# Transposed copies of x and context in DRAM, and the keys contracted over rows of 512 weights

## The reference

```python
def reference(x, ctx_4096, g_xattn, g_ffn, ...):
    def _L0_xattn_ref(text, features, Wq_w, Wq_b, Wk_w, Wk_b, fn_w, qn_w, kn_w):
        features_n = rmsnorm(features, fn_w)
        Q = jnp.einsum('btd,fd->btf', text, Wq_w) + Wq_b
        K = jnp.einsum('bsd,fd->bsf', features_n, Wk_w) + Wk_b
        Q = rmsnorm(Q, qn_w)
        K = rmsnorm(K, kn_w)
        scores = jnp.einsum('btf,bsf->bts', Q, K) * scale
        attn = jax.nn.softmax(scores, axis=-1)
        return jnp.einsum('bts,bsf->btf', attn, features_n)
    def _L0_ffn_ref(x, ...):
        base = jnp.einsum('bsd,od->bso', x, W_base) + b_base
        ...
        return base + moe.reshape(base.shape)
    x = x + jnp.tanh(g_xattn[0]) * _L0_xattn_ref(_layernorm(x, axis=-1), ctx_4096, ...)
    x = x + jnp.tanh(g_ffn[0]) * _L0_ffn_ref(_layernorm(x, axis=-1), ...)
    return x
```

## Time and profile before

| | us |
|---|---|
| median of 3 runs | 528.93 |
| lowest and highest | 528.06, 531.78 |
| the profiled execution, its own time | 526.89 |
| its span, first to last instruction | 525.1 |

### The profile page before, as it was taken

How to read it: one execution, slowest core, us unless ns; L and a number is a source line. 1 busy time by engine, 2 the same in 40 slices (tenths; PEclk the granted TensorE clock), 3 DMA queues, 4 the chain that set the end, 5 groups by cost and what they waited for, 6 DMA issues and landing times.

```text
span 525.1 us, 7062 instructions
## 1 busy us (share of the span) xinstructions
PE 500.9 (95%) x2768; PEld 459.6 (88%) x2768; DVE 271.2 (52%) x584; ACT 153.0 (29%) x323; POOL 153.4 (29%) x123
## 2 busy tenths in 40 slices
PE   2589999999999999999988999999999999999997
PEld 2589888888888888888888999999999999999997
DVE  3887543525352532156568766456554565654423
ACT  4476444243223322354541112211112111111100
POOL 3456566312222221145273320122201222012200
PEclk9799999999999999999999999999999999999999
DMA  8643611111112001321550322113221112210012
GB/s 316 256 157 114 240 41 41 41 41 40 41 40 81 1 1 64 139 71 51 201 161 32 90 80 81 41 40 122 80 81 52 41 69 81 82 41 38 3 41 81
DMA packets 11617, 43.51 MB, mean 83 GB/s; under 512 B 1600, under 2 KB 1984, under 8 KB 11200
## 3 DMA queue, kind: packets, MB, share of 16 engines
q1 hardware_dynamic: 11584, 43.06, 22.6%
HBM read 34.67 MB, written 8.39 MB: 82 GB/s over the span
## 4 chain that ended last, share of the span: by engine, by line
PE 81%; DVE 10%; DMA 3%; POOL 2%; ACT 2%; issue 2%; SPq 0%; POOLq 0%; DVEq 0%; ACTq 0%
PE bank L399 11%; PE bank L401 11%; PE bank L400 11%; PE bank L467 10%; PE bank L468 10%; PE bank L466 10%; PE bank L332 6%; DMA bb<-b_base_dram 2%; PE bank L480 2%; DVE xn L710 2%; DVE small L697 1%; PE bank L482 1%; PE bank L481 1%; PE bank L417 1%; PE bank L416 1%
## 5 line engine op out<-in xcount | busy, mean ns | idle before, releaser
L466 PE MATMUL bank<-wch,zth 128*128 128x388 f32 x384 | 132.5, 345 | 0.0
L467 PE MATMUL bank<-wcl,zth 128*128 128x388 f32 x384 | 130.5, 340 | 0.0
L468 PE MATMUL bank<-wch,ztl 128*128 128x388 f32 x384 | 129.8, 338 | 0.0
L399 PE MATMUL bank<-xth,wqh 128*128 128x512 f32 x256 | 102.1, 399 | 0.0
L401 PE MATMUL bank<-xth,wql 128*128 128x512 f32 x256 | 100.0, 390 | 0.0
L400 PE MATMUL bank<-xtl,wqh 128*128 128x512 f32 x256 | 99.8, 390 | 0.0
L899 POOL TENSOR_TENSOR small<-small,mhalf 128x1 f32<-128x1 f32 (+1 forms) x42 | 25.8, 615 | 218.8 <-DVE small L702 190.2
L773 DVE SCALAR_TENSOR_TENSOR qtl<-bank,vecs,qth 128x512 fp32r<-128x512 f32 x32 | 24.0, 750 | 100.5 <-ACT sq L630 100.5
L466 PEld LDWEIGHTS bank<-wch,zth 128*128 128x128 f32 x384 | 72.2, 188 | 1.0
L467 PEld LDWEIGHTS bank<-wcl,zth 128*128 128x128 f32 x384 | 72.3, 188 | 0.6
L468 PEld LDWEIGHTS bank<-wch,ztl 128*128 128x128 f32 x384 | 72.1, 188 | 0.0
(11 more groups left out here) (113 smaller groups left out, 642.3 us busy)
## 6 DMA issues: line engine op xcount, KB each, us to landing
x<-x_dram SPq DMA_DIRECT2D x32, 512.0 KB, 3.3
out_dram<-x SPq DMA_DIRECT2D x15, 512.0 KB, 2.6
wc_raw<-wc_dram SPq DMA_DIRECT2D x3, 1552.0 KB, 6.1
wk_raw<-wk_dram SPq DMA_DIRECT2D x8, 512.0 KB, 10.6
wq_raw<-wq_dram SPq DMA_DIRECT2D x8, 512.0 KB, 5.5
fn_raw<-ctx_dram SPq DMA_DIRECT2D x8, 256.0 KB, 5.0
ctx_raw<-ctx_dram SPq DMA_DIRECT2D x2, 512.0 KB, 3.7
fnw<-fn_w_dram SPq DMA_DIRECT2D x1, 512.0 KB, 6.4
```

The lines of the kernel that those rows point to most:

```text
L399: pe.matmul(acc[:, :], wqh[f][:, k, :], xth[b % 2][:, k, :], start=k == 0, stop=False)
L466: pe.matmul(acc, zth[z][:, k, :], wch[c][:, k, :], start=k == 0, stop=False)
L467: pe.matmul(acc, zth[z][:, k, :], wcl[c][:, k, :], start=False, stop=False)
L468: done = pe.matmul(acc, ztl[z][:, k, :], wch[c][:, k, :], start=False, stop=k == KB - 1)
```

## The change

The host lays out x a second time as `xt` (batch, 128 rows of features, 8 blocks of them, 512 tokens) and the context as `ctxt`; Wk comes transposed, as 8 rows of blocks of 128 inputs and 1024 features. The transposes of x and of the context go. In their place:

- Keys: `ct` splits the transposed context, weighted with fn_w, in four pieces; stage `k` now takes input block k, and for two halves of the context and two halves of 512 features makes 3 matmuls each (12 of 512 columns a k, four banks held through all eight k). Only when all are done does `k_norm` scale the sums by the context's norms (`ct_norm`), add the bias, take the norms of the keys and scale; then 16 transposes (`kt`) and eviction, copy and subtraction bring them to `kt`.
- Queries: `xstat` takes mean and variance of each tile of x in its rows. After the four tiles of a batch (`mr`) POOL takes the root, SP stores the 1024 numbers of 4 bytes to DRAM (`bounce`), waits, and loads them back spread over all 128 partitions (`mr`). `z` then centres and scales each quarter of `xt_raw` with them and splits it into `xth`/`xtl`. For batch 0 the DVE does this for quarters 0 and 1, POOL centres and scales 2 and 3; in later batches POOL centres and the DVE scales. `xt_raw` and `mr` exist once.
- qth and qtl get a third buffer; fnw is loaded late.

The diff, cut to its core:

```diff
+        first = [("ct", 0), ("wk", 0), ("k", 0), ("xstat", 0), ("xstat", 1), ("ct", 1), ("wk", 1), ("k", 1),
+                 ("xstat", 2), ("xstat", 3), ("mr", 0), ("ct", 2), ("ct", 3), ("wk", 2), ("k", 2), ("ct_norm",),
+                 ("wk", 3), ("k", 3), ("z", 0, 0), ("wk", 4), ("k", 4), ("z", 0, 2), ("wk", 5), ("k", 5), ("z", 0, 1),
+                 ("wk", 6), ("k", 6), ("wq", 0), ("z", 0, 3), ("wk", 7), ("k", 7), ("small",), ("wq", 1), ("k_norm",)]
...
+                if b == 0 and f == 1:
+                    first += [("kt", st, g) for st in range(2) for g in range(2)]
...
+                if b + 1 < B and 3 <= f < 7:
+                    first.append(("z", b + 1, f - 3))
                 if b + 1 < B:
-                    first += [("xt", (b + 1) * TPB + u // NH, u % NH) for u in XT_AT[f]]
...
+                if stage == "kt":
+                    st, g = i
+                    acc = ring_open((stage, st, g), "dve")
+                    if g == 0:
+                        pe.wait_ge(v_kn, st + 1)
+                    transposes(acc, kn_sb[st][:, g * HALF:(g + 1) * HALF].rearrange("p (j d) -> p j d", j=4))
...
+                    for st in range(2):
+                        s_cols = slice(st * P, (st + 1) * P)
+                        for h in range(NH):
+                            acc, cols = bank[K_BANKS[2 * st + h]], slice(h * HALF, (h + 1) * HALF)
+                            pe.matmul(acc[:, :], cth[:, k, s_cols], wkh[k][:, cols], start=k == 0, stop=False)
+                            pe.matmul(acc[:, :], cth[:, k, s_cols], wkl[k][:, cols], start=False, stop=False)
+                            done = pe.matmul(acc[:, :], ctl[:, k, s_cols], wkh[k][:, cols], start=False,
+                                             stop=k == KB - 1)
...
             sp.dma_start(vecs[:, :, :], vec).then_inc(ld_vec, 16)
+            load_ct(0)
+            load_wk(0)
+            load_x(0)
+            load_x(1)
+            load_ct(1)
+            load_wk(1)
+            load_x(2)
+            load_x(3)
+            load_ct(2)
+            load_ct(3)
+            load_wk(2)
+            load_wk(3)
+            load_xt(0, 0)
+            load_wk(4)
+            load_xt(0, 2)
+            load_wk(5)
+            load_xt(0, 1)
+            load_wk(6)
+            load_xt(0, 3)
+            load_wq(0)
+            load_wk(7)
+            load_wq(1)
+            sp.dma_start(bkb[:, :], bk_row.to_broadcast([P, D])).then_inc(ld_bk, 16)
+            sp.dma_start(sc[:, 0:3], scal.to_broadcast([P, 3])).then_inc(ld_sc, 16)
+            sp.wait_ge(v_xstat, TPB)
+            load_wq(2)
+            load_wq(3)
+            load_x(TPB)
+            load_x(TPB + 1)
...
+                if stage == "mr":
+                    b, = i
+                    sp.wait_ge(g_mr, b + 1)
+                    with nc.allow_non_contiguous_dma(reason="1024 statistics"):
+                        sp.dma_start(bounce.ap()[b].rearrange("(k j p) -> p k j", k=2, j=TPB),
+                                     ms[b % 2][:, :, :]).then_inc(st_mr, 16)
+                    if b > 0:
+                        sp.wait_ge(v_zl, 4 * b)
+                    sp.wait_ge(st_mr, 16 * (b + 1))
+                    sp.dma_start(mr[:, :, :].rearrange("p k t -> p (k t)"),
+                                 bounce.ap()[b:b + 1, :].to_broadcast([P, 2 * TB])).then_inc(ld_mr, 16)
+                    if b > 0:
+                        for c in range(4):
+                            load_xt(b, c)
+                elif stage == "q" and tuple(i) == (0, 0):
+                    sp.wait_ge(p_k, KB)
+                    for f in range(NWQ, FB):
+                        load_wq(f)
+                elif stage == "xstat" and TPB <= i[0] < NT - NXA:
+                    t, = i
+                    sp.wait_ge(v_xstat, t + 1)
...
+                elif stage == "z":
+                    b, c = i
+                    kc = slice(CK * c, CK * c + CK)
+                    act.wait_ge(*Z_READY[b, c])
+                    if b == 1:
+                        act.wait_ge(p_k, KB)
+                    elif b > 1:
+                        act.wait_ge(p_q, nq(b - 2, FB - 1) + 1)
+                    act.activation(xth[b % 2][:, kc, :], xt_raw[:, kc, :], ACT.Copy).then_inc(a_zh, 1)
+                elif stage == "k_norm":
+                    for st in range(2):
+                        act.wait_ge(v_kev, 2 * st + 2)
+                        act.activation(ct_raw[:, 4 * st:4 * st + 4, :], kn_sb[st][:, :].rearrange("p (a c) -> p a c", a=4),
+                                       ACT.Square, accum_out=k_ss[:, st:st + 1]).then_inc(a_ksq, 1)
+                elif stage == "kt":
+                    st, g = i
+                    f4, b2 = slice(4 * g, 4 * g + 4), slice(2 * st, 2 * st + 2)
+                    act.wait_ge(v_kraw, 2 * st + g + 1)
+                    for j in range(4 * g, 4 * g + 4):
+                        done = act.activation(kt[:, j, b2, 0:S], kt_raw[:, j, b2, S:P], ACT.Copy)
+                    done.then_inc(a_kth, 1)
...
+                elif stage == "z":
+                    b, c = i
+                    kc = slice(CK * c, CK * c + CK)
+                    z, m, r = xt_raw[:, kc, :], *(mr[:, k:k + 1, :].to_broadcast([P, CK, TB]) for k in range(2))
+                    if b == 0 and c < 2:
+                        if c == 0:
+                            dve.wait_ge(ld_mr, 16)
+                        dve.wait_ge(ld_xt[c], 16)
+                        dve.tensor_tensor(z, z, m, ALU.subtract).then_inc(v_zc, 1)
+                        dve.wait_ge(v_zc, c + 1)
+                        dve.tensor_tensor(z, z, r, ALU.mult).then_inc(v_z, 1)
+                    elif b > 0:
+                        dve.wait_ge(g_zc, 2 + (b - 1) * 4 + c + 1)
+                        dve.tensor_tensor(z, z, r, ALU.mult).then_inc(v_z, 1)
+                    dve.wait_ge(a_zh, Z_LOW[b, c])
+                    dve.tensor_tensor(xtl[b % 2][:, kc, :], z, xth[b % 2][:, kc, :].bitcast(F32),
+                                      ALU.subtract).then_inc(v_zl, 1)
...
+                elif stage == "k_norm":
+                    dve.wait_ge(p_k, KB)
+                    dve.wait_ge(ld_bk, 16)
+                    dve.wait_ge(g_ct, 1)
+                    for st in range(2):
+                        for h in range(NH):
+                            cols = slice(h * HALF, (h + 1) * HALF)
+                            dve.scalar_tensor_tensor(out=kn_sb[st][:, cols], in0=bank[K_BANKS[2 * st + h]][:, :],
+                                                     scalar=ct_rs[:, st:st + 1], in1=bkb[:, cols], op0=ALU.mult,
+                                                     op1=ALU.add).then_inc(v_kev, 1)
+                    dve.wait_ge(a_ksq, 2)
+                    dve.tensor_scalar(k_var, k_ss, 1.0 / D, RMS_EPS, ALU.mult, ALU.add).then_inc(v_kvar, 1)
+                    dve.wait_ge(g_krs, 1)
+                    for st in range(2):
+                        dve.tensor_scalar(kn_sb[st][:, :], kn_sb[st][:, :], k_rs[:, st:st + 1], None,
+                                          ALU.mult).then_inc(v_kn, 1)
+                elif stage == "kt":
+                    st, g = i
+                    f4, b2 = slice(4 * g, 4 * g + 4), slice(2 * st, 2 * st + 2)
+                    dve.wait_ge(p_ring, ring.full((stage, st, g)))
+                    if st == g == 0:
+                        dve.wait_ge(v_small, 2)
+                    for j in range(4 * g, 4 * g + 4):
+                        done = dve.tensor_scalar(
+                            kt_raw[:, j, b2, S:P],
+                            bank[T_BANKS[ring.number[stage, st, g] % 2]][:, (j - 4 * g) * P:(j - 4 * g + 1) * P].rearrange(
+                                "p (b s) -> p b s", b=2), kw[:, j:j + 1], None, ALU.mult)
+                    done.then_inc(v_kraw, 1)
+                    dve.wait_ge(a_kth, 2 * st + g + 1)
+                    for j in range(4 * g, 4 * g + 4):
+                        done = dve.tensor_tensor(kt[:, j, b2, S:P], kt_raw[:, j, b2, S:P],
...
+                elif stage == "z" and (i[0] > 0 or i[1] >= 2):
+                    b, c = i
+                    kc = slice(CK * c, CK * c + CK)
+                    z, m, r = xt_raw[:, kc, :], *(mr[:, k:k + 1, :].to_broadcast([P, CK, TB]) for k in range(2))
+                    pool.wait_ge(ld_mr, 16 * (b + 1))
+                    pool.wait_ge(ld_xt[c], 16 * (b + 1))
+                    pool.tensor_tensor(z, z, m, ALU.subtract).then_inc(g_zc, 1)
+                    if b == 0:
+                        pool.wait_ge(g_zc, c - 1)
+                        pool.tensor_tensor(z, z, r, ALU.mult).then_inc(g_z, 1)
```

495 lines of the change are left out of this document (214 added, 281 removed).

## The result

The changed kernel takes 586.34 us (median of 4 runs, 585.55 to 586.93) where the kernel before takes 529.17 on the same chip: a ratio of 1.107, with a 95% interval of 1.103 to 1.112. It is slower by 57 us. The profiled execution took 585.98, its span is 584.2.

What follows compares the result with a forecast made beforehand. TensorE, busy 95% of the span, bounds the kernel before. First query +30.2, batch 0 +20.4, batches 1 and 2 +2.0, batch 3 +2.4 make +55.0 on the span of 525.1, 580.1; forecast 582 us, range 555 to 600.

Steps and rivals of the forecast that it cites:

- The queue until 36.7: Start: SP's 22 blocks of 512 KB and smaller loads, issued ahead of the statistics' store, land at 36.7 us.
- bounce early: Rival, chance 0.18: the statistics' store does not wait behind queued loads; mr lands at 25.0, 18.1 sooner: 564 us.
- The store's own price, 1.5: Start: writing 1024 statistics of 4 bytes to DRAM takes 1.5 us, taken between bounds of 0 and 10.2.
- dear elements: Rival, chance 0.12: the store of 1024 elements takes 10.2 us in place of 1.5, +8.7: 591 us.
- The load of `mr`, 4.8: Start: loading the statistics back spread over 128 partitions takes 4.8 us: 3.3 with 2.8 for 1.27.
- M: Start: the time at which batch 0's mr lands, forecast as 36.7 + 1.5 + 4.8 + 0.1 = 43.1 us.
- From M to the first query, 34.1 + 2.4: Start: z and key weight splits through the last key take 34.1 us, half clock 2.4 more; first query at 79.6.
- Batch 0, 71.7: First query batch: matmuls 47.0, transposes 2.0, waits 9.3 + 1.5 + 9.8 + 2.1 make 71.7 us, +20.4.
- Batches 1 and 2, 54.1 each: Middle query batches: 53.1 less 3.7 for transposes, plus waits of 2.4 and 2.3, make 54.1 us, +1.0 each.
- The gain, 3.7 a batch: Query batches 0 to 2: removing 8 transpose groups of x at 0.46 us each saves TensorE 3.7 us a batch.
- the clock: Rival, chance 0.14: four waits among q4 to q7 each lower TensorE's clock, costing 2.2 us each, 9 in all: 591 us.
- TensorE stays the bound: Rival, chance 0.05: first query at 33.6, batches of 49.0, 49.4, 49.4 and 51.1; 25.5 us less, 501 us.

Runs made afterwards that it cites:

- e1: Changed kernel with each batch's statistics stored as 128 rows of 32 bytes instead of 1024 elements of 4 bytes (tokens get others' statistics): 571.24 us, ratio 1.079.
- e2: Changed kernel with batch 0's statistics store issued right behind the load of wk 4, and mr's load behind that of wk 5: 571.19 us, ratio 1.079.
- e6: Changed kernel with all of batch 0's z subtraction and product on VectorE, none on GpSimd: 582.96 us, ratio 1.102.
- e7: Changed kernel with the splits and matmuls of key weight rows 4 to 7 ahead of batch 0's four z pieces: 576.22 us, ratio 1.091.
- e10: e9 with the context's norms behind z, z's pieces in order between the last key weights' splits, and keys' groups moved: 542.15 us, ratio 1.030.
- e5: Kernel before without the 16 transpose groups of x for batches 2 and 3 (their queries read earlier batches' tiles): 522.23 us, ratio 0.988.
- e4: Changed kernel with ScalarE's copy of z and VectorE's low half one feature block behind the product in batches 1 to 3: 573.68 us, ratio 1.083.
- e9: Changed kernel with statistics transposed on TensorE and stored as 8 rows of 512 bytes, plus the edits of e2, e3, e4 and e7: 552.1 us, ratio 1.046.
- e11: e10 with four places mended: batch 1's statistics transpose later, last key weight earlier, query weights' splits in blocks 0 to 2, keys' groups moved: 534.59 us, ratio 1.014.
- e3: Changed kernel with batch 0's four keys' transposed groups put two behind block 0 and two behind block 1, ahead of x's statistics: 581.7 us, ratio 1.101.
- e12: e11 with the keys' groups of batches 0 and 1 ahead of batch 1's statistics, whose transpose and z come later: 540.35 us, ratio 1.021.

## Why the prediction was right, and where its steps were not

The forecast was 582 with a range of 555 to 600; 586.3 was measured. The path was right: `mr` late behind the queue, the key weights' splits behind `mr`, then the two loops of batch 0. The sum is closer than its parts, and that is luck: on the span +4.9 for `mr`, -1.7 for the chain behind it, -3.0 for batch 0, +0.8 and +2.0 for batches 1 and 2, -0.3 for batch 3 and +1.4 for the second half make +4.1. The parts, in order:

- **The queue until 36.7: right.** With a cheap store in its place (e1) the store landed at 38.2, the very 36.7 + 1.5 of the text. The rival "bounce early" fell: the store landed at 44.65, and 38.2 with the cheap one.
- **The store's own price, 1.5: wrong, and the one step that failed by much.** It is 8 us more than for few rows (10.3 alone), near the upper bound of 10.2 that the earlier trace rows gave and that the rival "dear elements" used. The Trainium skill's sentence ("DMA: Bandwidth & Descriptors", Rules for kernel authors) that a strided last dimension becomes one descriptor per element agrees with the packets counted in e1, where 128 rows in place of 1024 elements took the 8 us away. I had taken the value near the lower end because of the one tiny transfer in the trace, which has 128 packets, not 1024. By e2, the loads behind it are held up as well. So it was the rival's condition that came true. Its 591 is 4.7 too high and the forecast's 582 is 4.3 too low: half of the rival's excess is its 10.2 where 8.0 was measured, half the smaller terms below.
- **The load of `mr`, 4.8:** 3.3 (44.65 to 48.0), just what the plain block took in the earlier trace rows; the 1.5 added for its being spread over the partitions was not there. So M was 48.0 instead of 43.1: +6.4 - 1.5.
- **From M to the first query, 34.1 + 2.4:** 29.7 to the last low half (31.4 forecast) and 5.1 for the last key at half clock (2.7 + 2.4): 82.8 instead of 79.6. The turns of VectorE and GpSimd were as described. How much of the chain's length they are stays open, since e6 left nearly as many of them on the VectorE. That the order of the list holds the keys and the first query back is shown by e7 and e10.
- **Batch 0, 71.7:** 68.7. The keys' wait of 9.3 was measured as 9.3, with a group every 2.9 us. The z loop's period was 9.5, not 10.4, and it and the query weights' splits made TensorE wait 5.2 (4.3 on `wql`, 0.9 on `qtl`), not 9.8 + 1.5. The lowered clock cost more than the 2.1: TensorE's busy time is 54.2 where 49.0 was reckoned at full clock. The two errors partly cancel.
- **Batches 1 and 2, 54.1 each:** 54.9 and 56.1. The loop's period was 7.2 (7.9 forecast), but late pieces of z, by the dear stores, gave that back and more: with cheap stores they were 52.1 and 52.0.
- **Batch 3:** +2.1 (+2.4 forecast); the second half +1.4, which was not forecast. Its 1511 matmuls are busy for 259.8 us instead of 258.3: TensorE waits 3.1 us at `L915` (2.5 in the kernel before), and behind that the granted clock is 0.50 from 336 to 338, where the kernel before keeps 1.00.
- **The gain, 3.7 a batch:** 3.5 by e5. It is in the changed kernel too, under its waits: once those are gone (e4, e9, e11) a batch takes 49.7 to 50.5 where 53.0 was.
- The rival "the clock" was borne out once in place of four times: batches 1 to 3 ran at a clock of 1.00. In batch 0 it was 0.50 from 100 to 109 us, behind the wait of 7.5 for the keys' groups, and again from 144 to 147, in the z loop, behind waits of 0.9 and 2.2. "TensorE stays the bound" fell with `mr` at 48.

So the answer to "why slower" is: waiting, not work. Of the 59 us, 31.4 are key weights behind `mr`, shown by e7 (the order), e1 and e2 (`mr` itself). TensorE is busy 2.6 us more, the span is 59 longer. By medians the store's elements are worth 15 us (e1), its place in the queue 15 (e2), the z loop 13 (e4), the order of the splits 10 (e7); these overlap and don't add up. Together, with the last mends of the order, they are worth 52 us (e11), or 49 by the two ratios, since e11 ran on a chip on which the kernel before is 2.3 us faster.

## What to carry to other kernels

A step that goes through DRAM and back stands in three orders at once: that of the engine that computes it, that of the issuing engine's queue, and that of the lists of all engines that consume it; ahead of an in-order engine, what matters is what stands behind the waiting instruction. Before taking work off a busy engine, price the substitute's latency and its number of elements, not its bytes. A loop through several engines costs its full round trip per step unless its halves are put a step apart; that edit alone gave 12.7 us here for no work at all. Where one engine's list is the long chain over a stretch, moving work within it shifts the wait and gains little (e3, e12).

## What was not expected of the hardware

- 1024 elements of 4 bytes (4 KB) written to DRAM took 10.3 us alone, 128 rows of 32 bytes 2.1, 8 rows of 512 bytes 1.3; two loads issued right behind the elements crept at 48 to 8 GB/s until they were out (e2), against 414 in the earlier trace rows. The load issued just ahead of the store completed late too: 20.5 us after its issue at 24.0, but 14.0 in e1, though its bytes had moved by 38.
- The lock between VectorE and GpSimd also holds for tiny instructions: four subtractions of 128 columns took 4.85 to 6.08 us instead of 0.9 beside GpSimd's splits of 1024. Single ones took up to 2.4 us where 0.28 is usual, about the length of one split.
- Reading a broadcast operand with a step of 8 words made a VectorE product of 1024 columns 2.12 us instead of 1.22, and GpSimd's subtraction 3.07 instead of 2.39.
- With some 4.5 MB of loads still to land (about nine of 512 KB), SyncE took 1.08 us to issue one DMA, where a lone issue takes 0.38 (the store's two rows above). The statistics were ready at 17.9, but the issues ahead of it, of 1 us and more each, let the store be issued only at 25.1, at no cost here, as the queue was full in any case.
